# Four key-rounding steps moved from the end of a batch into the first three pairs of the next

## Chip, cores and metric

One Trainium2 chip, one core. The metric is the device time of one execution in microseconds, lower is better.

## What is computed

Two layers of gated cross-attention with a feed-forward part each, on x of 32 batches x 100 rows x 256, with a context of 32 x 1444 x 64. The change lies in the second layer's attention (sixteen heads), which per batch is, cut:

```python
kv_r = _apply_rope(kv_c, sin_k[None], cos_k[None])
q_r = jnp.einsum('bshq,hqr->bhsr', q_big, W_qr)
k_r = jnp.einsum('bld,hdr->bhlr', kv_r, W_kr)
scores = jnp.einsum('bhsr,bhlr->bhsl', q_r, k_r)
attn = jax.nn.softmax(scores, axis=-1)
ctx_c = jnp.einsum('bhsl,bld->bhsd', attn, kv_r)
```

The kernel folds W_kr into the queries, so that all heads share the 64-wide keys kv_r.

## The kernel before

The second attention (`phase_l1_attention`) runs eight groups of G = 4 batches. A group has a head, which makes the queries of its four batches and prepares batch 0's keys, and then a body in which four batches follow one another. In the body each batch has two chunks of 800 queries and twelve tiles of 120 or 121 keys in each chunk, so 24 tiles w, taken two at a time: 12 **pairs** per batch, here numbered 0 to 11. Pair p has the tiles 2p and 2p + 1. The text calls the four batches of a group 0 to 3, and the stretch between two of them a transition (into batch 1, 2 or 3).

All engines walk the same list of pairs, each with its own instruction stream, in the order written:

- **TensorE (PE)**, per pair: the scores of two tiles into c_s_ps (L1674 for the row maxima where r < 2, then L1676, L1678, L1680), a few "units" of the row maxima of the next batch (L1587), the values of the pair before (L1692), more units. Scores are three products, because each key is split in a rounded part k1 and a remainder k2, each held twice, on partitions 0 to 63 and on 64 to 127.
- **ScalarE (ACT)**, per pair: four exps c_s_ps to c_p (L1508); now and then the copies of the outputs (`drain`, L1473) and of the sums of the denominators (L1479); then, in two halves, the "rise" units of the maxima (L1456), with the **rounding steps** after the rises of the first half.
- **GpSimd (POOL)**, per pair: c_psum, the sum of the two exp tiles (L1194); at some pairs also the rotation of later keys (L1150, L1153, L1159) and the differences c_kd (L1174).
- **VectorE (DVE)**, per pair: the "low" and "mid" units of the maxima (L1271, L1277), then the accumulation of c_psum in c_acc (L1313, L1316), and at pairs 9, 10 and 11 one third of the split of the next keys (`split_keys`, L1267).

The maxima units come as rise, low and mid, each in one of three PSUM banks; TensorE may use a bank again when ScalarE (rise) or VectorE (low, mid) has read it. Exps of pair u wait for GpSimd's add of pair u - 2.

The nine rounding steps of a batch are in `round_steps` (L1458). Steps 0, 1, 2 write the rounded keys' three thirds to partitions 0 to 63 of k1, steps 3, 4, 5 the same to partitions 64 to 127 (both L1463, from c_kd); steps 6, 7, 8 copy the three thirds of the remainder k2 to the upper partitions (L1467), each after VectorE's L1267 for that third. The steps count up the semaphores k1_hi and k2_ready. `TILE_STEPS` (L971) says behind which tile of the batch before each step runs. Of those who wait: VectorE's third k waits for step k. TensorE's scores wait in `scores`, in the first chunk:

```python
if c == 0 and r % 4 == 0:
    pe.wait_ge(k1_hi, PRIMED + (it * G + j) * 6 + 4 + r // 4)
    pe.wait_ge(k2_ready, PRIMED + (it * G + j) * 3 + 1 + r // 4)
```

so the scores of pair 0 (r = 0) need steps 0 to 3 and 6, those of pair 2 (r = 4) steps 4 and 7, and those of pair 4 (r = 8) steps 5 and 8. `copy_keys` (L1440) overwrites c_kd with the next batch's keys, before the differences and the steps; it runs at pair 4 of batches 0 and 1, at pair 3 of batch 2, and in the head.

Of the kernel before, what the change touches and what calls it, by code (L numbers as in the profile page):

```python
# [15 lines left out]
G = 4  # L16
# [19 lines left out]
PRIMED = 1  # L36
# [3 lines left out]
def keys_of(r):  # L40
    return KP if r < 4 else KP - 1
# [796 lines left out]
def phase_l1_attention(nc, outer, sem, io, m):  # L838
# [12 lines left out]
    CT = CH * NT  # L851
    HEADS = [2 * i for i in range(H // 2)] + [2 * i + 1 for i in range(H // 2)]
    HALFQ, QUART = CQS // 2, CQS // 4
    with ExitStack() as ctx:
# [4 lines left out]
        def count(name):  # L859
            counters.append(sem(name))  # L860
            return counters[-1]
# [39 lines left out]
        kd_ready, k1_hi, k1_ready, k2_ready = count("c_kd_ready"), count("c_k1_hi"), count("c_k1_ready"), count("c_k2_ready")  # L901
# [15 lines left out]
        def beside_head(i):  # L917
            if i == HEAD_DEN:
                return ("den", -1)
            if i == HEAD_KEYS:  # L920
                return ("keys", 0)
            if i in HEAD_MAX:
                return ("max", 0, 0, HEAD_MAX.index(i))
            return ("none",)
# [43 lines left out]
        AFTER_PROJECT = {next_in(2, units_at(j, 15).start): j for j in range(1, G - 1)}  # L968

        HEAD_STEPS = {10: (0, 1), 11: (2,), 12: (3,), 13: (4, 5), 15: (6, 7, 8)}  # L970
        TILE_STEPS = {16: (0,), 17: (1,), 18: (2,), 19: (3,), 20: (4,), 21: (5,), 22: (6,), 23: (7,)}  # L971

        def pairs():
            for u in range(NP):
                yield u, u // BP, u // CP % CH, u % CP

        def head_cols(i):
            h = HEADS[i]
            return slice((h % 2) * CQS + (h // 2) * S, (h % 2) * CQS + (h // 2 + 1) * S)

        with nc.Block() as block:
# [448 lines left out]
            @block.scalar  # L1430
            def _(a):
                def copy_queries(gi, pair, src):
                    a.wait_ge(q_ps_ready, PRIMED + gi * (H // 2) + pair + 1)
                    a.sem_inc(m.carrier, 1)
                    for i in range(2):
                        for half in range(2):
                            a.activation(q1[half * DL:(half + 1) * DL, :, head_cols(2 * pair + i)],  # L1437
                                         src[i * DL:(i + 1) * DL, 0:T].rearrange("p (b s) -> p b s", b=G), ACT.Copy).then_inc(q1_ready, 1)

                def copy_keys(b):  # L1440
                    for k in range(3):
                        a.wait_ge(kt_ready, PRIMED + b * 3 + k + 1)
                        a.activation(kd[:, k * 4 * KP:(k + 1) * 4 * KP], m_ps[0:DL, k, 0:4 * KP], ACT.Copy).then_inc(kf_ready, 1)
                    a.activation(khigh[:, 0, :], m_ps[0:DL, 1, 0:4 * KP], ACT.Copy).then_inc(kmax_high, 1)

                def rise_tile(gi, t):
                    a.wait_ge(maxs_ready, PRIMED + gi * NMG + 3 * t + 3)
                    a.wait_ge(mneg_ready, PRIMED + gi * TG + t - 1)
                    a.activation(head_rises[t % 2], m_ps[:, 0, 0:4 * KP], ACT.Relu).then_inc(rise_ready, 1)

                def rise_unit(it, n):
                    j, k = divmod(n, NMU)
                    t, kind, half = UNITS[k]
                    a.wait_ge(maxs_ready, PRIMED + it * NMG + n + 1)
                    a.wait_ge(mneg_ready, PRIMED + it * TG + j * NMT + t - 1)
                    a.activation(rises[(j * NMT + t) % 2], m_ps[:, n % 3, 0:4 * KP], ACT.Relu).then_inc(rise_ready, 1)  # L1456

                def round_steps(b, j, n):  # L1458
                    cols = slice(n % 3 * 4 * KP, (n % 3 + 1) * 4 * KP)
                    if n < 6:  # L1460
                        a.wait_ge(kd_ready, PRIMED + (b + 1) * 5)
                        a.sem_inc(m.carrier, 1)
                        a.activation(k1[j % 2][n // 3 * DL:(n // 3 + 1) * DL, cols], kd[:, cols], ACT.Copy).then_inc(k1_hi, 1)  # L1463
                    else:
                        a.wait_ge(k1_ready, PRIMED + b * 3 + n - 5)
                        a.sem_inc(m.carrier, 1)
                        a.activation(k2[j % 2][DL:128, cols], k2[j % 2][0:DL, cols].bitcast(F32), ACT.Copy).then_inc(k2_ready, 1)  # L1467

                def drain(ch):

                    a.wait_ge(pv_done, PRIMED + (ch + 1) * NT)
                    a.wait_ge(ct_ready, PRIMED + ch)
                    a.activation(onum[:], o_ps[:, 0:HALFQ], ACT.Copy).then_inc(on_ready, 1)  # L1473

                def drain_sums(ch):
                    a.wait_ge(den_done, PRIMED + ch + 1)
                    a.wait_ge(den_loaded, 16 * ch)
                    a.sem_inc(m.carrier, 1)
                    a.activation(oden[:], m_ps[:, 0, 0:QUART], ACT.Copy).then_inc(od_ready, 1)  # L1479

                def head(gi, prev):
                    for i in range(H):
                        if i >= 3 and i % 2 == 1:
                            copy_queries(gi, i // 2 - 1, o_ps)
                        what, *at = beside_head(i)
                        if what == "den" and prev:
                            drain_sums(gi * G * CH - 1)
                        if what == "keys":
                            copy_keys(gi * G)
                        if what == "max":  # L1490
                            rise_tile(gi, at[2])
                        for n in HEAD_STEPS.get(i, ()):
                            round_steps(gi * G, 0, n)
                def group(it):
                    a.activation(warm[:], m.ident[0:1, 0:1], ACT.Exp)
                    for u, j, c, q in pairs():
                        ch, k = (it * G + j) * CH + c, keys_of(2 * q)
                        for w in range(2 * u, 2 * u + 2):
                            n = it * NU + w
                            for i in range(2):  # L1500
                                a.wait_ge(s_ready, PRIMED + 2 * n + i + 1)
                                if w >= 4:
                                    a.wait_ge(pv_done, PRIMED + n - 3)
                                    a.wait_ge(psum_ready, PRIMED + it * NP + u - 1)
                                else:
                                    a.wait_ge(pv_done, PRIMED + it * NU)
                                    a.wait_ge(psum_ready, PRIMED + it * NP)
                                a.activation(p[0:k, w % 4, i * HALFQ:(i + 1) * HALFQ], s_ps[0:k, (2 * w + i) % 4, 0:HALFQ], ACT.Exp).then_inc(exp_ready, 1)  # L1508
                        if (j, c) != (0, 0) and q == 0:
                            drain(ch - 1)  # L1510
                        for half in range(2):
                            for what, at in beside(j, u % BP * 2 + half):
                                if what == "absorb":
                                    copy_queries(it, H // 2 - 1, m_ps[:, 2, :])
                                if what == "den":
                                    drain_sums(it * G * CH + at)
                                if what == "keys":
                                    copy_keys(it * G + at)
                            for n in units_at(j, u % BP * 2 + half):
                                if UNITS[n % NMU][1] == "rise":  # L1520
                                    rise_unit(it, n)
                            if half == 0:
                                for w in range(2 * u, 2 * u + 2):
                                    for n in TILE_STEPS.get(w % CT, ()) if j + 1 < G else ():
                                        round_steps(it * G + j + 1, j + 1, n)
                                    if w % CT == 1 and j > 0:
                                        round_steps(it * G + j, j, 8)
                    drain((it * G + G) * CH - 1)

                head(0, False)  # L1530
                with a.Fori(0, NG - 1) as it:
                    group(it)
                    head(it + 1, True)
                group(NG - 1)
                drain_sums(B * CH - 1)

# [640 lines left out]
```

## Time and profile before

| | us |
|---|---|
| median of 3 runs | 3296.32 |
| lowest, highest | 3287.39, 3297.56 |
| the profiled execution | 3302.86 |
| its span (first to last instruction) | 3301.1 |

Busy shares of that span: TensorE 86%, its weight loads (PEld) 58%, VectorE 69%, ScalarE 50%, GpSimd 50%. The granted TensorE clock is 0.932 of full speed on average.

How to read it: times in the timeline are us from the start of the span. A row gives the start, the length from the first instruction of the row to the end of the last, the engine, the line of the kernel, what it writes and reads, and how many instructions the row holds. In brackets stands how long the engine was idle before the row and what ended that. "<-issue" means that nothing in the profile shows what it waited for. PEld rows are TensorE's weight loads; the load is the first thing of a matmul to start.

### The profile page before, as it was taken

What the parts mean: (1) busy time and instruction counts of PE and PEld (TensorE: products, weight loads), DVE (VectorE), ACT (ScalarE), POOL (GpSimd) and SP (SyncE); (2) the same over time, 40 slices, a digit from 0 to 9 for tenths busy, and PEclk for the clock granted to TensorE, in tenths of its full rate; (3) what the DMA queues carried; (4) which work ended last, traced back from release to release, by engine and by line L of the source; (5) the groups of instructions that cost most, each with busy time, mean ns of one, the idle gap of its engine ahead of it and who ended that gap; (6) DMA issues with size and microseconds to landing.
All of it is one profiled execution on the core that took longest, in us unless ns stands there. A gap on an engine that the chain in (4) does not pass through costs nothing. (4 is left out here: it accounts for less than half of the span.)

```text
span 3301.1 us, 62826 instructions
## 1 busy us (share of the span) xinstructions
PE 2836.6 (86%) x18352; PEld 1917.0 (58%) x18352; DVE 2270.5 (69%) x4122; ACT 1658.6 (50%) x3458; POOL 1637.5 (50%) x1196
## 2 busy tenths in 40 slices
PE   5999979999798998898998999899899899886335
PEld 4777769999665565565555555556556556553123
DVE  5777764454376686677677667768767667766887
ACT  2333222222146646646646655655664664664556
POOL 0000012322166656666666666665665666663566
PEclk9888879999899999999999999999999999998566
DMA  4000010000300101000000000010110000011100
GB/s 112 0 0 0 0 48 10 5 10 10 75 6 21 26 10 23 19 16 17 21 21 16 22 19 17 16 26 7 23 23 11 22 19 16 11 48 35 44 13 24
DMA packets 130264, 71.20 MB, mean 22 GB/s; under 512 B 83582, under 2 KB 124510, under 8 KB 129880
## 3 DMA queue, kind: packets, MB, share of 16 engines
q1 hardware_dynamic: 129944, 67.45, 8.2%
q8 instruction: 138, 2.26, 0.3%
q14 instruction: 182, 1.49, 0.1%
HBM read 56.95 MB, written 10.04 MB: 20 GB/s over the span
## 5 line engine op out<-in xcount | busy, mean ns | idle before, releaser
L1194 POOL TENSOR_TENSOR c_psum<-c_p 120x800 f32<-120x800 f32 (+1 forms) x384 | 770.8, 2013 | 558.8 <-ACT c_p L1508 240.1
L1508 ACT ACTIVATE c_p<-c_s_ps 120x400 f32<-120x400 f32 (+1 forms) x1536 | 650.5, 512 | 331.8 <-PE c_s_ps L1680 258.7
L1692 PE MATMUL c_o_ps<-c_p,c_val 120*64 120x400 f32 (+1 forms) x3072 | 605.1, 516 | 10.9 <-ACT c_onum L1473 10.9
L1271 DVE TENSOR_REDUCE c_mpart<-c_m_ps 128x1 f32<-128x484 f32 x416 | 271.4, 653 | 203.6 <-PE c_m_ps L1587 203.1
L1587 PE MATMUL c_m_ps<-c_kmax,c_q 64*128 64x484 f32 x1080 | 308.5, 437 | 98.6 <-DVE c_mpart L1271 63.6
L1316 DVE TENSOR_TENSOR c_acc<-c_acc,c_psum 120x800 f32<-120x800 f32 x256 | 319.3, 1247 | 59.9 <-POOL c_psum L1194 57.9
L1185 POOL TENSOR_TENSOR l_rr<-c_psum,l_rr 96x400 f32<-96x400 f32 x256 | 263.6, 1052 | 191.0 <-DVE l_rr L1338 190.9
L1692 PEld LDWEIGHTS c_o_ps<-c_p,c_val 120*64 120x64 f32 (+1 forms) x3072 | 188.8, 137 | 273.5 <-issue 159.7
L1676 PE MATMUL c_s_ps<-c_q,c_k 64*120 64x400 f32 (+1 forms) x1536 | 322.9, 370 | 1.8 <-ACT c_p L1508 1.8
L1623 PE MATMUL c_s_ps<-c_xt,l_a 128*96 128x400 f32 x1536 | 310.8, 352 | 9.7 <-DVE l_rr L1338 7.8
L1277 DVE CUSTOM_DVE_ANT_0 c_xt<-c_m_ps,c_xt,c_mpart 128x484 fp32r<-128x484 f32 x360 | 259.9, 722 | 86.0 <-DVE c_mpart L1271 42.1
L1587 PEld LDWEIGHTS c_m_ps<-c_kmax,c_q 64*128 64x128 f32 x1080 | 144.3, 187 | 288.3 <-issue 157.9
L1680 PE MATMUL c_s_ps<-c_q,c_k 64*120 64x400 f32 (+1 forms) x1536 | 302.1, 346 | 0.0
L1678 PE MATMUL c_s_ps<-c_q,c_k 64*120 64x400 f32 (+1 forms) x1536 | 301.6, 346 | 0.0
L1623 PEld LDWEIGHTS c_s_ps<-c_xt,l_a 128*96 128x96 f32 x1536 | 240.2, 162 | 88.7 <-issue 42.6
L528 POOL TENSOR_TENSOR b_act_lo<-b_act,b_act_hi 128x400 fp32r<-128x400 f32 x88 | 92.0, 1050 | 293.7 <-ACT b_act_hi L672 293.7
L717 PE MATMUL b_gu_ps<-b_xt,l_a 128*128 128x400 f32 x1056 | 212.9, 353 | 8.0 <-DVE b_gated L563 7.9
L1456 ACT ACTIVATE c_xt<-c_m_ps 128x484 fp32r<-128x484 f32 x360 | 193.9, 587 | 48.0 <-PE c_m_ps L1587 31.9
L717 PEld LDWEIGHTS b_gu_ps<-b_xt,l_a 128*128 128x128 f32 x1056 | 195.4, 194 | 12.2 <-DVE b_gated L563 12.0
L1676 PEld LDWEIGHTS c_s_ps<-c_q,c_k 64*120 64x120 f32 (+1 forms) x1536 | 163.0, 181 | 67.4 <-issue 37.5
L1437 ACT ACTIVATE c_q<-c_o_ps 64x400 fp32r<-64x400 f32 x224 | 112.0, 500 | 176.9 <-PE c_o_ps L1613 172.8
L1678 PEld LDWEIGHTS c_s_ps<-c_q,c_k 64*120 64x120 f32 (+1 forms) x1536 | 173.2, 182 | 4.0
(258 smaller groups left out, 5212.1 us busy)
## 6 DMA issues: line engine op xcount, KB each, us to landing
c_rdb<-l_denominators SPq DMA_DIRECT2D x128, 100.0 KB, 2.7
c_kv<-in_ctx SPq DMA_DIRECT2D x32, 360.0 KB
c_mrow<-c_mneg SPq DMA_DIRECT2D x288, 0.5 KB, 2.0
x_rows<-in_x SPq DMA_DIRECT2D x4, 800.0 KB
x_spill<-x_rows SPq DMA_DIRECT2D x8, 400.0 KB
l_xa<-x_spill SPq DMA_DIRECT2D x8, 400.0 KB
c_xr<-x_spill SPq DMA_DIRECT2D x32, 100.0 KB
x_spill<-c_xr SPq DMA_DIRECT2D x32, 100.0 KB
```

The costliest lines, as they stand in the source:

```text
L717: mm = pe.matmul(gu_ps[:, t % 2, j, 0:T], w[wi][:, k, t * 128:(t + 1) * 128], xt[x][:, k, :], start=(i == 0 and k == 0), stop=(i == 2 and ...
L1185: g.tensor_tensor(rot[:, i % 4, a, :], psum[0:HALF, i % 2, a * T:(a + 1) * T], rs[:, i % 2, (1 - a) * T:(2 - a) * T], ALU.add).then_inc(ro ...
L1194: g.tensor_tensor(psum[0:k, u % 2, :], p[0:k, 2 * u % 4, :], p[0:k, (2 * u + 1) % 4, :], ALU.add).then_inc(psum_ready, 1)
L1271: v.tensor_reduce(mpart[:, t:t + 1], m_ps[:, bank, 0:4 * KP], AX.X, ALU.max, negate=True).then_inc(mpart_ready, 1)
L1316: v.tensor_tensor(acc[0:k, :], acc[0:k, :], psum[0:k, q % 2, :], ALU.add).then_inc(acc_ready, 1)
L1508: a.activation(p[0:k, w % 4, i * HALFQ:(i + 1) * HALFQ], s_ps[0:k, (2 * w + i) % 4, 0:HALFQ], ACT.Exp).then_inc(exp_ready, 1)
L1587: pe.matmul(m_ps[:, n % 3, 0:4 * KP], q1[rows, j, q], kmax[rows, 1 if kind == "rise" else 0, :], start=True, stop=True).then_inc(maxs_read ...
L1623: mm = pe.matmul(wide_banks(i)[0:HALF, a, 0:T], m.a[w][:, k, HEADS[i], a * HALF:(a + 1) * HALF], xt[x][:, k, :], start=(q == 0 and k == 0) ...
L1676: pe.matmul(bank[i][0:k], k1[j % 2][side[i], keys], q1[side[i], j, q[i]], start=False, stop=False, skip_group_check=True)
L1678: pe.matmul(bank[i][0:k], k2[j % 2][side[i], keys], q1[side[i], j, q[i]], start=False, stop=False, skip_group_check=True)
L1680: pe.matmul(bank[i][0:k], k1[j % 2][side[i], keys], q2[side[i], j, c, :], start=False, stop=True, skip_group_check=True).then_inc(s_ready, 1)
L1692: mm = pe.matmul(o_ps[i * DL:(i + 1) * DL, 0:HALFQ], val[0:k, j % 2, r, :], p[0:k, w % 4, i * HALFQ:(i + 1) * HALFQ], start=(r == 0), stop ...
```

## The change

Steps 4, 7, 5 and 8 of a batch's keys go to the first three pairs of that batch itself; steps 0, 1, 2, 3 and 6 stay in the last four pairs of the batch before, one in pairs 8, 9 and 11 and two in pair 10. `copy_keys` gets a wait for all six k1 steps of the keys before. Batch 0's keys, which are rounded in the head, keep their steps.

```diff
-        TILE_STEPS = {16: (0,), 17: (1,), 18: (2,), 19: (3,), 20: (4,), 21: (5,), 22: (6,), 23: (7,)}
+        TILE_STEPS, LATE_STEPS = {16: (0,), 18: (1,), 20: (2,), 21: (3,), 23: (6,)}, {1: (4,), 3: (7,), 4: (5,), 5: (8,)}
...
                 def copy_keys(b):
+                    a.wait_ge(k1_hi, PRIMED + b * 6)
                     for k in range(3):
...
                                     for n in TILE_STEPS.get(w % CT, ()) if j + 1 < G else ():
                                         round_steps(it * G + j + 1, j + 1, n)
-                                    if w % CT == 1 and j > 0:
-                                        round_steps(it * G + j, j, 8)
+                                    for n in LATE_STEPS.get(w % CT, ()) if j > 0 else ():
+                                        round_steps(it * G + j, j, n)
```

| pair | 8 | 9 | 10 | 11 | 0 | 1 | 2 |
|---|---|---|---|---|---|---|---|
| steps before | 0, 1 | 2, 3 | 4, 5 | 6, 7 | 8 | | |
| steps after | 0 | 1 | 2, 3 | 6 | 4 | 7 | 5, 8 |

## Rows read from the trace of the kernel before

**Rows 1.** The page: its first line and the busy shares.

```profile
span 3301.1 us, 62826 instructions
PE 2836.6 (86%) x18352; PEld 1917.0 (58%) x18352; DVE 2270.5 (69%) x4122; ACT 1658.6 (50%) x3458; POOL 1637.5 (50%) x1196
```

**Rows 2.** Groups by line, whole span: count, busy us, mean ns, idle before, releasers.

```profile
L1267 DVE TENSOR_TENSOR c_k<-c_kd,c_k 64x484 fp32r<-64x484 f32 x96 | 91.2, 962 | 0.0
L1467 ACT ACTIVATE c_k<-c_k 64x484 fp32r<-64x484 f32 x96 | 54.7, 601 | 13.3 <-DVE c_k L1267 12.1
```

**Rows 3.** Timeline of ScalarE, pairs 8 to 11 of batch 2: start, length, row.

```profile
2173.30 1.11 ACT L1463 ACTIVATE c_k<-c_kd 64x484 fp32r<-64x484 f32 x2
...
2178.52 1.69 ACT L1508 ACTIVATE c_p<-c_s_ps 120x400 f32<-120x400 f32 x4 [0.83 <-PE c_s_ps L1680]
...
2186.49 0.60 ACT L1467 ACTIVATE c_k<-c_k 64x484 fp32r<-64x484 f32 x1 [1.73 <-DVE c_k L1267]
2187.12 1.06 ACT L1456 ACTIVATE c_xt<-c_m_ps 128x484 fp32r<-128x484 f32 x2
```

**Rows 4.** Timeline of ScalarE, pair 10 of batch 0 and ahead of pair 11 of batch 1.

```profile
2070.87 1.69 ACT L1508 ACTIVATE c_p<-c_s_ps 120x400 f32<-120x400 f32 x4 [1.02 <-POOL c_psum L1194]
...
2130.24 0.58 ACT L1456 ACTIVATE c_xt<-c_m_ps 128x484 fp32r<-128x484 f32 x1 [1.29 <-DVE c_mneg L1277]
```

**Rows 5.** Timeline of TensorE's weight loads, from batch 2 into batch 3.

```profile
2186.72 0.18 PEld L1587 LDWEIGHTS c_m_ps<-c_kmax,c_q 64*128 64x128 f32 x1 [1.08 <-DVE c_mpart L1271]
2187.24 0.19 PEld L1674 LDWEIGHTS c_s_ps<-c_mrow,c_first 64*121 64x121 f32 x2 [0.34 <-ACT c_k L1467]
```

**Rows 6.** Timeline of VectorE, pairs 9 to 11 of batch 2.

```profile
2178.96 1.67 DVE L1316 TENSOR_TENSOR c_acc<-c_acc,c_psum 120x800 f32<-120x800 f32 x1
2180.55 2.37 DVE L1267 TENSOR_TENSOR c_k<-c_kd,c_k 64x484 fp32r<-64x484 f32 x1
...
2185.45 0.65 DVE L1267 TENSOR_TENSOR c_k<-c_kd,c_k 64x484 fp32r<-64x484 f32 x1
```

**Rows 7.** Timeline of ScalarE and weight loads, pairs 1 to 3 of batch 1.

```profile
2088.38 1.70 ACT L1508 ACTIVATE c_p<-c_s_ps 121x400 f32<-121x400 f32 x4
...
2090.68 0.18 PEld L1676 LDWEIGHTS c_s_ps<-c_q,c_k 64*120 64x120 f32 x2 [0.32 <-issue]
...
2094.28 1.04 ACT L1456 ACTIVATE c_xt<-c_m_ps 128x484 fp32r<-128x484 f32 x2 [0.99 <-PE c_m_ps L1587]
2095.21 1.70 ACT L1508 ACTIVATE c_p<-c_s_ps 120x400 f32<-120x400 f32 x4
```

**Rows 8.** Timeline of ScalarE and weight loads, pairs 1 and 2 of batch 2.

```profile
2139.01 1.69 ACT L1508 ACTIVATE c_p<-c_s_ps 121x400 f32<-121x400 f32 x4
...
2141.64 0.18 PEld L1676 LDWEIGHTS c_s_ps<-c_q,c_k 64*120 64x120 f32 x2 [0.32 <-issue]
```

**Rows 9.** Timeline of ScalarE and weight loads, pairs 1 and 2 of batch 3.

```profile
2193.44 1.07 ACT L1456 ACTIVATE c_xt<-c_m_ps 128x484 fp32r<-128x484 f32 x2
...
2194.74 0.18 PEld L1676 LDWEIGHTS c_s_ps<-c_q,c_k 64*120 64x120 f32 x2 [0.32 <-issue]
```

**Rows 10.** Timeline of both, sixth group, from batch 0 into batch 1.

```profile
2344.88 1.10 ACT L1467 ACTIVATE c_k<-c_k 64x484 fp32r<-64x484 f32 x2
...
2345.88 0.19 PEld L1674 LDWEIGHTS c_s_ps<-c_mrow,c_first 64*121 64x121 f32 x2 [0.47 <-ACT c_k L1467]
```

**Rows 11.** Timelines of GpSimd and ScalarE, pairs 3 and 4 of batch 3.

```profile
2199.51 1.69 ACT L1508 ACTIVATE c_p<-c_s_ps 120x400 f32<-120x400 f32 x4 [2.10 <-POOL c_psum L1194]
...
2200.92 3.75 POOL L1194 TENSOR_TENSOR c_psum<-c_p 120x800 f32<-120x800 f32 x2 [1.44 <-DVE c_acc L1313]
...
2202.86 1.69 ACT L1508 ACTIVATE c_p<-c_s_ps 120x400 f32<-120x400 f32 x4 [1.66 <-POOL c_psum L1194]
```

**Rows 12.** Timelines of GpSimd and VectorE, pairs 2 to 4 of batch 1.

```profile
2095.73 3.76 POOL L1194 TENSOR_TENSOR c_psum<-c_p 120x800 f32<-120x800 f32 x2 [1.29 <-ACT c_p L1508]
...
2098.91 1.42 DVE L1316 TENSOR_TENSOR c_acc<-c_acc,c_psum 120x800 f32<-120x800 f32 x1
```

## The prediction

> **What bounds the kernel now.** Read first the page's busy shares [rows 1]: TensorE is busy 86% of the span, ScalarE 50%. So a ScalarE step that moves is worth nothing by itself; it counts only where TensorE is made to wait for it, or is let go by it. Next come the costs of the pieces, from the groups by line [rows 2]: a rounding step of the last kind (L1467, steps 6 to 8) is 0.60 us, and L1267, the VectorE split between them, has a mean of 0.96 us. Only L1467 has idle time before it worth naming, 13.3 us, nearly all on L1267.
>
> Then the timeline of one group of four batches, the fifth (it starts at 2030). The eight groups repeat each other within some tenths of a us, so a place in it counts eight times. Each group has three transitions that the change touches, into batches 1, 2 and 3; batch 0's keys are rounded in the head, which stays. I number the pairs of a batch 0 to 11. In every pair TensorE's scores come first, and ScalarE does its four exps, the rises of the first half, then the rounding steps, then the rises of the second half.
>
> **Part 1: fewer steps in the last four pairs.** Before, pairs 8 to 11 carry two steps each and pair 0 of the next batch one. After, pairs 8 and 9 carry one, pair 10 two, pair 11 one. Gone from the end are steps 4, 5 and 7, three steps. If ScalarE were the bound this would give 3 x 0.5 us (two steps in a row take 1.11 us, [rows 3], so the second adds 0.5) x 24 transitions = 36 us. The rows say that it is not:
> - Into batch 1: behind the steps of pair 9, the exps of pair 10 start after 1.02 us of idle time that GpSimd's c_psum add ended [rows 4]. A step less only makes such a wait longer. Gain 0.
> - Into batch 2: ScalarE has no idle time behind the steps of pairs 8 and 9, so it may win up to 0.5 us in each, but ahead of pair 11's exps it waits 1.29 us, in a rise of pair 10, for VectorE's c_mneg [rows 4]; what it won is spent there. 0.
> - Into batch 3: the exps of pair 9 may win up to one step, 0.5 us, but those of pair 10 wait 0.83 us for TensorE [rows 3]: 0. In pair 11 step 7 waits 1.73 us for L1267 and holds the rises behind it until 2187.12 [rows 3]. After the change step 7 is not there, and the first rise can go some 1.1 us sooner. It is nobody's last wait: TensorE's last maxima in that pair waited for VectorE's c_mpart (1.08 us) and the scores of pair 0 come directly behind, at 2187.24 [rows 5].
> Gain 0. If the exps of pair 9 that ScalarE now holds back were worth something, I bound it by 0.2 us a group, 1.6 us: the rows that follow them all name another engine. What hides the steps here is VectorE, whose split L1267 takes 2.37 us in place of 0.65 while GpSimd adds [rows 6]. The split of each third still finds its step done: step 1 now ends a pair ahead of L1267's second piece, step 2 likewise ahead of the third.
>
> The Trainium skill has a rule on this (SBUF — State Buffer, section "Who interferes with whom"): only VectorE and GpSimd share a port pair, the loser blocks wholly, and ScalarE has ports of its own. By that rule the moved copies can't slow L1267 or the GpSimd adds directly, and 0.65 against 2.37 us is a lock and not ScalarE's doing; they can only shift who meets whom, which is the second and fourth case below.
>
> **Part 2: step 4 in place of step 8 in pair 0.** The same engine, place and length. 0.
>
> **Part 3: step 7 in pair 1.** This is the new cost. TensorE's scores of pair 2 (r = 4) wait for the second k2_ready, which is step 7. Before, it was done a pair before the batch began. Now ScalarE reaches it only behind pair 1's exps, and TensorE starts pair 2's scores about there. The step starts 0.03 us behind its predecessor (2187.09 to 2187.12, [rows 3]), takes 0.61, and TensorE's weight load follows its end by 0.15 us (2187.24 against 2187.09, [rows 3, 5]): 0.79 us in all.
> - Into batch 1: exps end at 2088.38 + 1.70 = 2090.08; + 0.79 = 2090.87; TensorE's load ran at 2090.68 [rows 7]. Late by 0.19.
> - Into batch 2: 2139.01 + 1.69 + 0.79 = 2141.49; the load ran at 2141.64 [rows 8]. Late by 0, and ScalarE was idle there.
> - Into batch 3: two rises lie between exps and step (slot 2 of batch 3 has rises in its first half). They end at 2193.44 + 1.07 = 2194.51; + 0.79 = 2195.30; the load ran at 2194.74 [rows 9]. Late by 0.56.
> Queued behind that wait on TensorE are the scores, maxima and values of pair 2, and VectorE and GpSimd behind those. Sum 0.75 us a group, x 8 = 6.0 us. The lag from step to load isn't the same everywhere: the longest I find is 2345.88 - (2344.88 + 0.60) = 0.40 us [rows 10], which gives 0.44 + 0.10 + 0.81 = 1.35 us a group, 10.8 us; a lag of 0.05 would give 0.09 + 0 + 0.46, 4.4 us. I take the 0.15 since it is of the same wait in the same group.
>
> Does the delay last? Into batch 3 the exps of pair 3 wait for GpSimd anyway, which would hide it. But VectorE's L1313, which comes behind pair 2's maxima, moves with TensorE; GpSimd's add waits 1.44 us for it, and the exps of pair 4 wait 1.66 us for that add [rows 11]. So the 0.56 us goes around and stays. If instead it is absorbed there, 1.5 us of the 6.0 remain.
>
> **Part 4: steps 5 and 8 in pair 2.** Needed for pair 4's scores, one pair of slack. Into batch 1 they take 1.1 us where ScalarE was idle 0.99 us before its rises [rows 7], so with the 0.19 of part 3 the rises and pair 3's exps come some 0.3 us later. Pair 4's scores need only the first of those exps, and come a pair later; 0. Cover gone, it would be 0.3 x 8 = 2.4 us.
>
> **Part 5: the added wait in copy_keys** (for all six L1463 of the batch before). Behind it on ScalarE are the copies to c_kd, behind those L1257 and the next maxima. The sixth step ran in pair 2, copy_keys comes in pair 3 or 4, and already waits there for TensorE's transposes. 0; an instruction more, below 0.1 us x 32 = 3 us were it not covered, my bound from the 0.03 us between neighbours [rows 3].
>
> **The sum.** 0 + 0 + 6.0 + 0 + 0 on the profiled execution's 3302.9 us (3301.1 us of span and 1.8 around it): 3308.9. That execution lies 6.6 us above the median of the runs, 3296.3, so I state 3296.3 + 6.0 = 3302.3 us, +0.18%. About 0.3%, 10 us, is what a measurement of this kernel can tell from no change.
>
> **The rivals.**
> 1. *Absorbed.* The 0.56 us of batch 3 vanishes in the waits for GpSimd (2.10 us of idle time ahead of pair 3's exps, [rows 11]), and part 1's 1.6 us comes in: 3296.3 + 1.5 - 1.6 = 3296 us. Against it stands the chain over L1313.
> 2. *A split escapes GpSimd: faster.* In pair 10 of batch 2, L1267 starts at 2180.55 behind the accumulation L1316, which is 1.67 us long under GpSimd's rotation of keys; GpSimd's next add starts when pair 10's exps end, 2178.52 + 1.69 = 2180.21, and L1267 takes 2.37 us under it in place of 0.65 [rows 3, 6]. If pair 9's exps come sooner, so do GpSimd's add and rotation, and from 0.4 us on L1267 would be first. VectorE then runs ahead by 1.72 us, and TensorE waited for it. Price at most -1.72 x 8 = -13.8, with part 3's 6.0 against it -7.8: 3288.5 us. ScalarE can give at most the 0.5 us of one step, and only if the scores were ready that early.
> 3. *No relation.* The wait for step 7 is hidden, because TensorE spends the 0.32 us ahead of that load on its own waits [rows 7 to 9] and the step ends inside them: as 1, 3296 to 3298 us.
> 4. *An accumulation falls under GpSimd: slower.* Into batch 1, late steps 5 and 8 push pair 3's exps. GpSimd's adds of pairs 2 and 3 run in one piece of 3.76 us until 2099.49, and VectorE's L1316 at 2098.91 overlaps only the end, 1.42 us long [rows 12]. If pair 3's exps end later than 2097.6, against 2095.21 + 1.70 = 2096.91 now [rows 7], the second add moves on and the accumulation takes up to 2.4 us: +1.0 x 8 = 8 on the 6.0: 3310 us. I expect 0.3 us of push, and 0.55 with the longest lag, so it takes more than I count. The 0.40 us lag everywhere gives nearly the same time, 3307.
>
> **Numbers.** Forecast, +4 to +11: 0.52. Rivals 1 and 3 together: 0.20. Rival 2: 0.12, rival 4: 0.16. The range reaches from rival 2's end to a little past rival 4: 3288 to 3313. Faster by over 0.3%: 0.13, a part of rival 2 and of what I don't see in the meeting of VectorE and GpSimd. Slower by over 0.3%: 0.22, rival 4 and the top of the forecast. Within: 0.65.
>
> **What would show it.** In the profile after: TensorE's load L1676 of pair 2 into batches 1 and 3 released by ScalarE's L1467, with idle time up to 0.5 and 0.9 us in place of 0.32, and not into batch 2; step L1467 in pair 11 of batch 2 followed at once by rises with no second L1467; exps of pairs 9 and 10 into batch 1 still released by c_psum; L1267's mean near 0.96 us. Wrong if L1267 or L1316 has another mean (rivals 2, 4), if pairs 8 to 11 get shorter by over 0.3 us, or if pair 2 doesn't get longer.

## The result and the profile after

The changed kernel was timed against the one before three times, each time in runs interleaved on one chip.

| timing | after, median us | before, median us | ratio, 95% interval |
|---|---|---|---|
| first | 3307.11 | 3293.66 | 1.0040 [1.0021, 1.0058] |
| again | 3304.44 | 3294.78 | 1.0033 [1.0014, 1.0052] |
| third | 3305.47 | 3297.19 | 1.0029 [1.0017, 1.0041] |

So the change makes the kernel slower, by 0.3 to 0.4%. Over all three, 30 executions of after have a mean of 3305.2 us and 110 of the kernel before (the unchanged copy of the last experiment among them) one of 3295.6: +9.5 us, plus or minus 2.3. The forecast was 3302.3 us, +6.0. The time falls in the range, the sign and the mechanism are as forecast, and the size is at the edge: +0.18% was forecast, with the chance on "within 0.3%", and the first timing says 0.4%. That the mean loss lies in the forecast's +4 to +11 us is in part luck, since about half of it stands in no term of the sum, as shown below.

The page of after, its first line and the busy shares, answers to [rows 1]:

```profile
span 3310.5 us, 62858 instructions
PE 2841.8 (86%) x18352; PEld 1921.9 (58%) x18352; DVE 2268.8 (69%) x4122; ACT 1661.0 (50%) x3458; POOL 1637.7 (49%) x1196
```

No engine got more to compute: 32 instructions came in (the waits of `copy_keys`). TensorE is busy 5.2 us longer with the same 18352 matmuls, and ScalarE 2.4 us. The profiled execution took 3312.5 us against 3302.9, but two later profiles of the same kernel have spans of 3296.4 and 3296.7 us, under the 3301.1 of before. A span by itself says nothing at this size; where the time went has to be read pair by pair. Lines from 1441 on are one higher in after and in the kernels made from it (L1468 is the L1467 of the rows before), and three higher in splits_later and best_of_both.

Groups by line, whole span, as in [rows 2]:

```profile
L1267 DVE TENSOR_TENSOR c_k<-c_kd,c_k 64x484 fp32r<-64x484 f32 x96 | 91.2, 962 | 0.0
L1468 ACT ACTIVATE c_k<-c_k 64x484 fp32r<-64x484 f32 x96 | 56.0, 599 | 1.2
```

The split keeps its mean of 962 ns to the digit: no sign that a split changed its place against GpSimd. The remainder steps, though, lost nearly all their idle time, 13.3 us before and 1.2 now: step 7 no longer waits in pair 11. That gain is real and bought nothing, as part 1 said. ScalarE in pair 11 of batch 2 shows it, where [rows 3] had step 7 behind 1.73 us of idle time:

```profile
2189.06 0.61 ACT L1468 ACTIVATE c_k<-c_k 64x484 fp32r<-64x484 f32 x1
...
2190.95 0.57 ACT L1457 ACTIVATE c_xt<-c_m_ps 128x484 fp32r<-128x484 f32 x1 [1.28 <-PE c_m_ps L1588]
```

One step, and then ScalarE waits 1.28 us for TensorE instead: the idle time has only changed its cause.

Now the pairs that got longer. Batch 3, ScalarE and TensorE in pairs 0 to 2, which answers to [rows 9]:

```profile
2196.16 0.61 ACT L1464 ACTIVATE c_k<-c_kd 64x484 fp32r<-64x484 f32 x1
2196.79 1.69 ACT L1509 ACTIVATE c_p<-c_s_ps 121x400 f32<-121x400 f32 x4
2198.35 1.07 ACT L1457 ACTIVATE c_xt<-c_m_ps 128x484 fp32r<-128x484 f32 x2
2199.18 0.55 PE L1594 MATMUL c_m_ps<-c_acc,c_ones 121*32 121x200 f32 x8 [0.37 <-ACT c_xt L1457]
2199.44 0.60 ACT L1468 ACTIVATE c_k<-c_k 64x484 fp32r<-64x484 f32 x1
2200.10 0.18 PEld L1677 LDWEIGHTS c_s_ps<-c_q,c_k 64*120 64x120 f32 x2 [0.76 <-ACT c_k L1468]
```

Step 7 runs behind the rises, from 2199.44 to 2200.04, and the load of pair 2's scores follows 0.06 us later, with 0.76 us of idle time that step 7 ended; before it was 0.32 us of issue. Batch 1 and batch 2, the same places, answer to [rows 7, 8]:

```profile
2093.10 1.70 ACT L1509 ACTIVATE c_p<-c_s_ps 121x400 f32<-121x400 f32 x4
2094.82 0.61 ACT L1468 ACTIVATE c_k<-c_k 64x484 fp32r<-64x484 f32 x1
2095.49 0.18 PEld L1677 LDWEIGHTS c_s_ps<-c_q,c_k 64*120 64x120 f32 x2 [0.39 <-ACT c_k L1468]
...
2143.91 1.69 ACT L1509 ACTIVATE c_p<-c_s_ps 121x400 f32<-121x400 f32 x4
2145.63 0.61 ACT L1468 ACTIVATE c_k<-c_k 64x484 fp32r<-64x484 f32 x1
2146.55 0.18 PEld L1677 LDWEIGHTS c_s_ps<-c_q,c_k 64*120 64x120 f32 x2 [0.32 <-ACT c_k L1468]
```

In batch 1 the idle time grew by 0.07 us. In batch 2 it is 0.32 us as before, and step 7 had ended at 2146.24, 0.31 us ahead of the load: the row names it, but it didn't hold the load.

To compare whole kernels I took, for each pair, the time from its first scores (the L1676 matmul) to those of the next pair, as a difference to before, and of the eight groups the median. For most pairs this repeats to 0.01 or 0.02 us between executions, where the time of an execution scatters by some 6 us. Two pairs do not repeat: pair 11 of batch 0 (5.4 to 6.4 us within before, and 0.13 us less for the unchanged kernel) and pair 0 of batch 1 (3.7 to 4.3 us within before). Pair 11 has a column of its own and is in no sum; pair 0 is in the sums, and 0.1 us of it means nothing. For all kernels of this text, us a group (a dash: under 0.03), with the timed difference at the end (ratio minus one, times 3295; for after the three values). Two slow executions, one of 4_and_7_in_pair1 (4575 us) and one of the kernel before (3653 us), are in no ratio.

| kernel | batch 0 pair 11 | batch 1 pair 0 | pair 1 | pair 3 | batch 3 pair 0 | pair 1 | elsewhere | sum x 8 | timed, 95% |
|---|---|---|---|---|---|---|---|---|---|
| after (three profiles) | -0.24 to 0 | 0 to +0.03 | +0.07 | +0.07 | - | +0.45 | - | +4.8 | +9.6 to +13.2 |
| step7_back | -0.11 | -0.10 | - | +0.07 | - | - | - | -0.2 | +4.6 (-2 to +11) |
| wait_alone | -0.25 | -0.06 | - | - | - | - | +0.04 | -0.2 | -3.3 (-8 to +2) |
| only_7_8 | -0.11 | -0.08 | - | - | - | +0.32 | - | +1.9 | +4.9 (-1 to +11) |
| 4_and_7_in_pair1 | +0.38 | +0.04 | +0.35 | +0.07 | - | +0.82 | +0.16 | +11.6 | +16.5 (+11 to +22) |
| 4_and_7_in_pair0 | -0.24 | - | +0.28 | +0.07 | - | +0.49 | - | +6.7 | +7.6 (+3 to +12) |
| splits_later | -0.17 | -0.08 | +0.54 | +0.07 | +1.23 | +0.49 | -2.68 | -3.3 | -6.6 (-12 to -1) |
| rotation_later | -0.07 | -0.12 | - | - | +0.78 | - | +3.42 | +32.6 | +33 (+26 to +40) |
| step8_to_pair2 | -0.14 | - | - | - | - | -0.14 | - | -1.1 | +1.0 (-3 to +5) |
| best_of_both | -0.15 | +0.55 | - | - | - | -0.14 | -2.23 | -14.5 | -15.2 (-20 to -10) |
| same_again | -0.13 | - | - | - | - | - | - | 0 | +1.3 (-4 to +6) |

### The profile page after: what moved, and what is told of

The parts are those of the page before. It is cut to its first block and busy times, and to the rows that moved or that the text cites. A ratio compares the mean times of both kernels' runs of the same rounds, so it can differ in the third digit from the quotient of the medians.

```text
span 3310.5 us, 62858 instructions
## 1 busy us (share of the span) xinstructions
PE 2841.8 (86%) x18352; PEld 1921.9 (58%) x18352; DVE 2268.8 (69%) x4122; ACT 1661.0 (50%) x3458; POOL 1637.7 (49%) x1196
## 5 line engine op out<-in xcount | busy, mean ns | idle before, releaser
L1316 DVE TENSOR_TENSOR c_acc<-c_acc,c_psum 120x800 f32<-120x800 f32 x256 | 317.3, 1239 | 59.9 <-POOL c_psum L1194 57.9
```

The source lines that it names most:

```text
L1316: v.tensor_tensor(acc[0:k, :], acc[0:k, :], psum[0:k, q % 2, :], ALU.add).then_inc(acc_ready, 1)
```

## The experiments

Each edit is against the kernel before or the changed one, as its first line says. The pair numbers are those of the table above.

**After, again, and step 7 back in its place.** The first asks whether the pair times repeat; the second, whether step 7 alone carries them.

> The changed kernel once more. Theory A (step 7 holds TensorE back ahead of pair 2; nothing else costs): the two traces show 0.45 us into batch 3 and 0.07 to 0.2 us into batch 1, about 4.4 us in eight groups, so a ratio of 1.0013 to before; the 1.004 measured first was then partly chance. Theory B (a further cost that the one trace doesn't show): 1.004 again, some 13 us.

```diff
 against the changed kernel, step7_back:
-TILE_STEPS, LATE_STEPS = {16: (0,), 18: (1,), 20: (2,), 21: (3,), 23: (6,)}, {1: (4,), 3: (7,), 4: (5,), 5: (8,)}
+TILE_STEPS, LATE_STEPS = {16: (0,), 18: (1,), 20: (2,), 21: (3,), 22: (6,), 23: (7,)}, {1: (4,), 4: (5,), 5: (8,)}
```

> The changed kernel with step 7 alone back in pair 11 of the batch before. Theory A: the load of pair 2 into batch 3 returns to its old distance, pair 1 there 0.45 us shorter than in the changed kernel, total equal to before within 1 us. Theory B (fewer steps at the end, or the wait in copy_keys, cost): stays at +8 us or more.

After again: 1.0033 [1.0014, 1.0052], with pair 1 of batch 3 longer by 0.44 us (0.45 in the first profile) and pairs 1 and 3 of batch 1 by 0.07 each. Step 7 back: 3302.08 us, 1.0014 [0.9994, 1.0033], and in batch 3, pairs 1 and 2:

```profile
2194.05 0.55 PE L1594 MATMUL c_m_ps<-c_acc,c_ones 121*32 121x200 f32 x8 [0.37 <-ACT c_xt L1457]
2194.52 0.18 PEld L1677 LDWEIGHTS c_s_ps<-c_q,c_k 64*120 64x120 f32 x2 [0.32 <-issue]
```

The load waits for nothing that the profile shows, as before, and the 0.45 is gone to the last hundredth. The timing of this kernel, 1.0014 with an interval from 0.9994 to 1.0033, tells it neither from before nor from after. So the finding rests on the pairs, and after timed again, 1.0033, speaks for the further cost of theory B. What is left of the change, steps 4, 5 and 8 in the next batch, costs 0.07 us a group, in pair 3 of batch 1, which appears in every kernel that has both steps 5 and 8 in pair 2 and in no other. Step 7 in pair 1 makes up nearly all of what the pairs gained.

**The wait alone, and only the steps of the remainder.** wait_alone is before with the wait in `copy_keys` and nothing else; only_7_8 leaves steps 4 and 5 in the batch before.

```diff
 against the kernel before, wait_alone:
 def copy_keys(b):
+    a.wait_ge(k1_hi, PRIMED + b * 6)
```

```diff
 against the changed kernel, only_7_8:
+TILE_STEPS, LATE_STEPS = {16: (0,), 17: (1,), 18: (2,), 19: (3,), 20: (4,), 21: (5,), 22: (6,)}, {3: (7,), 5: (8,)}
```

> The kernel before with only the added wait in copy_keys. Theory A: 0, below 1 us. Theory B, if the wait is its cause: +3 to +10 us.

> The changed kernel with steps 0 to 6 where they were before and only 7 and 8 late, in pairs 1 and 2. Theory A: into batch 3 the same 0.45 us, into batch 1 the same 0.1 or less, so +3.5 to +4.5 us over before, like the changed kernel. Theory B, if the cost is in steps 4 and 5: nearer 0.

The wait alone: 3293.87 us, 0.9990 [0.9975, 1.0006], and no pair longer by more than 0.04 us. Part 5's nothing holds. Only 7 and 8: 3297.97 us, 1.0015 [0.9998, 1.0033]; into batch 3:

```profile
2186.67 0.55 PE L1594 MATMUL c_m_ps<-c_acc,c_ones 121*32 121x200 f32 x8 [0.24 <-ACT c_xt L1457]
2186.94 0.60 ACT L1468 ACTIVATE c_k<-c_k 64x484 fp32r<-64x484 f32 x1
2187.59 0.18 PEld L1677 LDWEIGHTS c_s_ps<-c_q,c_k 64*120 64x120 f32 x2 [0.77 <-ACT c_k L1468]
```

The load waits 0.77 us for step 7, as in after (0.76), yet the pair is only 0.32 us longer and not 0.45. The rest is in the line above it: with no step in pair 0, the exps and rises of pair 1 come sooner, and the denominators' matmul L1594 waits 0.24 us for a rise in place of 0.37. So a step in pair 0 isn't free in batch 3 either. My part 3 had not seen this; the next two runs follow it.

**Steps 4 and 7 together, in pair 1 or in pair 0.**

```diff
 against the changed kernel, 4_and_7_in_pair1:
-TILE_STEPS, LATE_STEPS = {...}, {1: (4,), 3: (7,), 4: (5,), 5: (8,)}
+TILE_STEPS, LATE_STEPS = {...}, {3: (4, 7), 4: (5,), 5: (8,)}
 and 4_and_7_in_pair0:
+TILE_STEPS, LATE_STEPS = {...}, {1: (4, 7), 4: (5,), 5: (8,)}
```

> The changed kernel with step 4 moved from pair 0 to pair 1, right ahead of step 7, so that step 7 ends half a us later. Theory A (step 7's end sets pair 2's start): pair 1 gets longer than in the kernel before by 0.45 + 0.5 = 0.95 us in batch 3, by 0.07 + 0.5 = 0.57 in batch 1, and by some 0.3 in batch 2, where the slack ends: 1.8 us a group, +14.6 us to before, +10 to the changed kernel. Theory C (the delay is absorbed further on once it grows): the sum over the group stays below 1 us, +8.

> The changed kernel with step 7 moved from pair 1 to pair 0, behind step 4. Theory A: step 7 ends a pair ahead of its use, so pair 1 of batch 3 is as long as before, though all else of the change stays: 0 to before, at most +0.1 us a group from the exps of pair 1 starting 0.5 us later. Theory B (thinner last pairs or late 5 and 8 cost): +5 to +9 us to before as the changed kernel.

In pair 1: 3314.82 us, 1.0050 [1.0032, 1.0067]. ScalarE and TensorE, batch 3:

```profile
2198.33 0.60 ACT L1464 ACTIVATE c_k<-c_kd 64x484 fp32r<-64x484 f32 x1
2198.84 0.59 ACT L1468 ACTIVATE c_k<-c_k 64x484 fp32r<-64x484 f32 x1
...
2199.48 0.18 PEld L1677 LDWEIGHTS c_s_ps<-c_q,c_k 64*120 64x120 f32 x2 [1.26 <-ACT c_k L1468]
```

Step 7 starts 0.51 us behind step 4, and the load's idle time goes from 0.76 to 1.26: exactly one step more. (The pair grows by 0.82 - 0.45 = 0.37 us only, since no step is left in pair 0, which gives back 0.13 as in only_7_8.) The wait is on the path, and in batch 3 an instruction ahead of step 7 counts in full at the load. In batches 1 and 2 the pair grew by 0.35 and 0.16 us where 0.57 and 0.3 were expected, so the +14.6 of theory A came out as +11.6 in the pairs; timed it is +16.5, 11 to 22. In pair 0: 3305.28 us, 1.0023 [1.0010, 1.0035]. If only the end of step 7 mattered, this kernel would have cost nothing in batch 3, since step 7 is over two us before pair 2. It cost 0.49:

```profile
2187.59 0.61 ACT L1464 ACTIVATE c_k<-c_kd 64x484 fp32r<-64x484 f32 x1
2188.10 0.59 ACT L1468 ACTIVATE c_k<-c_k 64x484 fp32r<-64x484 f32 x1
2188.71 1.69 ACT L1509 ACTIVATE c_p<-c_s_ps 121x400 f32<-121x400 f32 x4
2190.27 1.07 ACT L1457 ACTIVATE c_xt<-c_m_ps 128x484 fp32r<-128x484 f32 x2
2191.10 0.55 PE L1594 MATMUL c_m_ps<-c_acc,c_ones 121*32 121x200 f32 x8 [0.86 <-ACT c_xt L1457]
2191.57 0.18 PEld L1677 LDWEIGHTS c_s_ps<-c_q,c_k 64*120 64x120 f32 x2 [0.32 <-issue]
```

Read it from the bottom: the load of pair 2 waits for nothing, but the matmul ahead of it in TensorE's order waits 0.86 us for a rise, 0.49 more than before. The rise stands directly behind the exps of pair 1, those directly behind the steps. That chain has no gap, so a second step in pair 0 is paid there, and one in pair 1 at the load. The theory that only step 7's end counts has fallen, for batch 3; the one in its place is that ScalarE itself bounds the first two pairs of batch 3, at 0.45 to 0.5 us a step. The +0.28 us in pair 1 of batch 1 is a third place of the same kind. There a rise of pair 0 stands directly behind step 7, which ends at 2083.88, and TensorE's next maxima unit needs its bank:

```profile
2083.91 1.04 ACT L1457 ACTIVATE c_xt<-c_m_ps 128x484 fp32r<-128x484 f32 x2
...
2084.53 0.18 PEld L1588 LDWEIGHTS c_m_ps<-c_kmax,c_q 64*128 64x128 f32 x1 [0.47 <-ACT c_xt L1457]
```

In the kernel before, the same two loads run directly one behind the other.

**What the end of a batch could give: splits a pair later, rotation later.** Both ask whether VectorE's collisions with GpSimd, and not ScalarE, hold pairs 10 and 11. splits_later moves L1267 from pairs 9, 10, 11 to pairs 10, 11 and pair 0 of the next batch. rotation_later moves GpSimd's rotation of keys from pairs 7 and 8 to 9 and 10.

```diff
 against 4_and_7_in_pair0, splits_later:
-if j + 1 < G and c == 1 and q >= 3:
-    split_keys(it * G + j + 1, j + 1, (q - 3,))
+if j + 1 < G and c == 1 and q >= 4:
+    split_keys(it * G + j + 1, j + 1, (q - 4,))
+if j > 0 and (c, q) == (0, 0):
+    split_keys(it * G + j, j, (2,))
 against the kernel before, rotation_later:
-if (more or j + 2 < G) and j + 1 < G and at in (7, 8):
-    rotate_keys(b + 2, at - 7)
+if (more or j + 2 < G) and j + 1 < G and at in (9, 10):
+    rotate_keys(b + 2, at - 9)
```

> The kernel with steps 4 and 7 in pair 0, and VectorE's three splits L1267 one pair later (pairs 10, 11 and 0 of the next batch in place of 9, 10, 11). Theory D (the first split runs under GpSimd's adds at 2.3 us in place of 0.65 into batches 1 and 3, and TensorE's 4.3 us stall in pair 10 of batch 0 hangs on it): L1267's mean falls from 0.96 to some 0.65 to 0.7 us, pair 10 of batch 0 gets shorter by 1.7 us or more and pair 11 of batch 2 by some 1.5: -3.2 x 8 = -26 us. Rival E (VectorE is behind there for another cause, the slow L1316): under -5 us.

> The kernel before with GpSimd's first two pieces of the key rotation (L1150, L1153) at pairs 9 and 10 in place of 7 and 8. Theory D': they no longer delay the adds of pairs 8 and 9 into batch 1, L1316 there falls from 2.5 to 1.0 us and the first split to 0.65, pair 10 of batch 0 gets shorter by 3 us: -24 us. Rival: the rotation meets VectorE's second and third splits and the accumulations of pairs 10 and 11 instead, and the time stays within 5 us or rises.

Splits later: 3289.67 us, 0.9980 [0.9965, 0.9996], faster than the 1.0023 of the same kernel without the edit by some 14 us. Theory D is right on pair 10 of batch 0 and on the split's mean (697 ns), but its -26 us did not come: -6.6 was measured. In the kernel before, pair 10 of batch 0 (VectorE, then TensorE's weight load):

```profile
2073.38 2.32 DVE L1267 TENSOR_TENSOR c_k<-c_kd,c_k 64x484 fp32r<-64x484 f32 x1
...
2076.33 0.28 PEld L1587 LDWEIGHTS c_m_ps<-c_kmax,c_q 64*128 64x128 f32 x1 [4.57 <-DVE c_mpart L1271]
```

and in splits_later, the same pair:

```profile
2061.26 2.50 DVE L1316 TENSOR_TENSOR c_acc<-c_acc,c_psum 120x800 f32<-120x800 f32 x1 [0.67 <-POOL c_psum L1194]
...
2064.38 0.18 PEld L1590 LDWEIGHTS c_m_ps<-c_kmax,c_q 64*128 64x128 f32 x1 [2.34 <-DVE c_mpart L1271]
...
2068.13 0.65 DVE L1267 TENSOR_TENSOR c_k<-c_kd,c_k 64x484 fp32r<-64x484 f32 x1
```

The accumulation is caught under GpSimd's work in both (2.50 us here, against 1.48 for the next one); before, the split came directly behind it, under GpSimd's adds, and TensorE's maxima waited for both, 2.32 us for the split. A pair later it takes 0.65, and TensorE's stall falls from 4.57 to 2.34 us: -2.23 a group. Pair 0 of batch 3 gives half of it back, 1.23 us. Step 6 waits for its split in pair 11 of batch 2 there, but that isn't the cause. The rows are step 6, then the first load of batch 3, and windows over its scores (us, busy and count of PE, PEld, DVE, ACT, POOL, granted clock, DMA share, GB/s):

```profile
2174.17 0.60 ACT L1470 ACTIVATE c_k<-c_k 64x484 fp32r<-64x484 f32 x1 [1.66 <-DVE c_k L1267]
...
2175.20 0.18 PEld L1677 LDWEIGHTS c_s_ps<-c_mrow,c_first 64*121 64x121 f32 x2 [0.34 <-issue]
...
2176.00:2178.20 2.20, 2.20 (x14) 1.68 (x12) 1.71 (x3) 1.33 (x4) 0.00 (x0) 0.50 0.07 1
```

The load doesn't wait for step 6: it idles 0.34 us as in [rows 5]. The clock is what changed: TensorE had idled for 1.82 us in pair 11 (0.79 in the kernel before), waiting for VectorE's c_mpart, and its scores behind that run at 0.50 of full speed. In seven of the eight groups this pair has a granted clock of 0.66 to 0.74 and is 1.04 to 1.58 us longer; in the eighth the clock stays at 1.00 and the pair is 0.01 us longer.

Rotation later: 3330.68 us, 1.0100 [1.0079, 1.0121], so the rival was right and theory D' not. The rotation then meets the splits head on; the group L1267 of this kernel is

```profile
L1267 DVE TENSOR_TENSOR c_k<-c_kd,c_k 64x484 fp32r<-64x484 f32 x96 | 126.0, 1325 | 0.0
```

a mean of 1325 ns in place of 962, 34.8 us in all, and the timed difference is 33 us. That the two are so near is in part chance: pair 0 of batches 2 and 3 is 1.2 to 1.6 us longer in four of the eight groups each, some 11 us together, each time at a granted clock of 0.65 to 0.71; where the clock is 1.00, all but one of these pairs are as long as before. Who meets whom on VectorE and GpSimd counts for more here than where a rounding step stands. The Trainium skill (SBUF — State Buffer, section "Who interferes with whom") has these two engines share a port pair under an exclusive lock. The 0.65 against 2.32 us of this case agree with it.

**Step 8 from pair 0 to pair 2, by itself.** If ScalarE bounds the start of batch 3, then taking the one step of pair 0 away should win what adding one cost.

```diff
 against the kernel before:
-if w % CT == 1 and j > 0:
+if w % CT == 5 and j > 0:
     round_steps(it * G + j, j, 8)
```

> The kernel before with step 8 alone moved, from pair 0 to pair 2, so that no step lies in pairs 0 and 1. Theory F (in batch 3 ScalarE's own chain from the output copy through pair 1's exps and rises sets TensorE's denominators matmul, and every step in pairs 0 and 1 costs its 0.5 us there): the 0.37 us that this matmul waits for the rises goes, pair 1 of batch 3 is 0.37 us shorter than before, total -3 us (-0.1%). Theory A (only step 7's own end matters): no change, 0.

3298.93 us, 1.0003 [0.9991, 1.0015]. The pair did get shorter, by 0.14 us and not by the 0.37 that the matmul's wait would have allowed. Its rows, pairs 1 and 2 of batch 3:

```profile
2183.55 1.69 ACT L1508 ACTIVATE c_p<-c_s_ps 121x400 f32<-121x400 f32 x4 [0.51 <-PE c_s_ps L1680]
...
2185.94 0.55 PE L1593 MATMUL c_m_ps<-c_acc,c_ones 121*32 121x200 f32 x8 [0.23 <-ACT c_xt L1456]
2186.41 0.18 PEld L1676 LDWEIGHTS c_s_ps<-c_q,c_k 64*120 64x120 f32 x2 [0.32 <-issue]
```

The matmul still waits for the rise, 0.23 us. But the exps at the head of the chain now wait 0.51 us for TensorE's scores, where in the kernel before they came directly behind step 8; they start 0.81 us behind the pair's first scores in place of 0.95. So the step was the last to hold them by 0.14 us only: a step more costs its whole length, a step less wins 0.14. That is why a bound found by adding work may not be read backwards.

**The best of both.** The splits later only into batch 1, where they paid; elsewhere as before; step 8 in pair 2; step 7 in pair 1 of batch 1 alone, since its split comes later there.

```diff
 against the kernel before:
+LATE_STEPS = {5: (8,)}
+FIRST_STEPS, FIRST_LATE = {w: n for w, n in TILE_STEPS.items() if w < 23}, {3: (7,), 5: (8,)}
+SPLITS, FIRST_SPLITS = {3: (0,), 4: (1,), 5: (2,)}, {4: (0,), 5: (1, 2)}
...
-if j + 1 < G and c == 1 and q >= 3:
-    split_keys(it * G + j + 1, j + 1, (q - 3,))
+if j + 1 < G and c == 1:
+    split_keys(it * G + j + 1, j + 1, (SPLITS if j > 0 else FIRST_SPLITS).get(q, ()))
...
-for n in TILE_STEPS.get(w % CT, ()) if j + 1 < G else ():
+for n in (TILE_STEPS if j > 0 else FIRST_STEPS).get(w % CT, ()) if j + 1 < G else ():
     round_steps(it * G + j + 1, j + 1, n)
-if w % CT == 1 and j > 0:
-    round_steps(it * G + j, j, 8)
+for n in (LATE_STEPS if j > 1 else FIRST_LATE).get(w % CT, ()) if j > 0 else ():
+    round_steps(it * G + j, j, n)
```

> Into batch 1: VectorE's splits in pairs 10, 11, 11, step 7 in pair 1, step 8 in pair 2, the other steps as before; into batches 2 and 3 the kernel before with step 8 in pair 2. Theory D and F: pair 10 of batch 0 shorter by 2.2 us, pair 1 of batch 3 by 0.37, L1267's mean near 0.77 us; -2.6 us a group, -21 us. Rival: the two splits in pair 11 give back what pair 10 gains, -3 to -8 us.

3278.90 us, 0.9954 [0.9939, 0.9970]: faster than both kernels. Groups by line and the stall of pair 10, batch 0:

```profile
L1270 DVE TENSOR_TENSOR c_k<-c_kd,c_k 64x484 fp32r<-64x484 f32 x96 | 77.2, 823 | 0.0
...
2061.01 0.18 PEld L1590 LDWEIGHTS c_m_ps<-c_kmax,c_q 64*128 64x128 f32 x1 [2.35 <-DVE c_mpart L1274]
...
2067.18 0.18 PEld L1677 LDWEIGHTS c_s_ps<-c_mrow,c_first 64*121 64x121 f32 x2 [1.86 <-issue]
2067.19 0.45 PE L1677 MATMUL c_s_ps<-c_mrow,c_first 64*121 64x400 f32 x2 [1.57 <-DMA c_mrow<-c_mneg]
```

The pairs add to -14.5 us (8 x (-2.23 + 0.55 - 0.14)), the timing says -15.2. The 0.55 us in pair 0 of batch 1 is the median of a wide scatter, 0.85 us shorter to 0.84 us longer; with pair 11 ahead of it that stretch takes 9.94 us in the mean of the eight groups, against 10.00 and 9.94 in the two profiles of the unchanged kernel. The last two rows are its next limit: in three groups, this one among them, TensorE comes to the head of batch 1 so early that its first matmul waits 1.57 to 1.71 us for the DMA that brings the row maxima, c_mrow.

**The control, and after a third time.** The unchanged kernel before, timed as if it were a change, and the changed one once more beside it.

> The kernel before, unchanged, as a control for what the timing can tell: 0, ratio 1.000 with an interval of about 0.002. Were it 1.001 or more, the 5 us between the changed kernel's runs and its trace would lie in the way of comparing.

> The changed kernel a third time, beside the control. Theory A or F: the pairs of its trace sum to +4 to +5 us, ratio 1.0015. Theory B: +10 us again, 1.003, with the control at 1.000.

The unchanged kernel: 3297.01 us, 1.0004 [0.9989, 1.0019], all pair medians under 0.03 us but pair 11 of batch 0. After: 3305.47 us, 1.0029 [1.0017, 1.0041], pairs as in its other two profiles. So what the comparison adds by itself is below 0.2%, and after's 0.3% is not of that kind. Theory A is right on the pairs and theory B on the time: there is a further cost that the pairs don't show. The two also show a place outside the groups where they differ, told below.

## Why the prediction was right or wrong

- **Part 1, nothing from the end of the batch: right.** Pairs 8 to 11 differ by 0.03 us or less in all three profiles of after, pair 11 of batch 0 left aside, which doesn't repeat. Step 7's 1.73 us wait vanished and nobody was waiting for it.
- **Part 2, step 4 for step 8: right** as an exchange. But the reason was incomplete: a step there is free in batches 1 and 2 and costs some 0.13 us in batch 3 (0.45 with it, 0.32 without).
- **Part 3, step 7 in pair 1: the mechanism right, the term too large.** Forecast 0.19, 0 and 0.56 us; the pairs grew by 0.07, 0 and 0.45. The step that missed is the lag from the end of step 7 to TensorE's load: I took 0.15 from another wait in the same group, where the step wasn't what the load waited for (that load idles 0.34 us in after too, with step 7 gone: 2192.14, "0.34 <-issue"), and it is 0.06 in both rows where step 7 is the last wait (2094.82 + 0.61 to 2095.49, 2199.44 + 0.60 to 2200.10). My lower end, a lag of 0.05, was the right row: it gave 4.4 us, and the pairs 1 of batches 1 and 3 add to 4.2. In batch 2 it was absorbed as forecast. The loads idle 0.39 and 0.76 us where I had said "up to 0.5 and 0.9".
- **The delay persists: right.** Over pairs 2 to 10 of batch 3 nothing is given back, against rival 1. The chain that I named carries it: in [rows 11] GpSimd's add waited 1.44 us for L1313 and the exps of pair 4 waited 1.66 us for that add; in after it is 1.91 and 2.12, some 0.46 us longer each.
- **Part 4, steps 5 and 8: nearly right.** Forecast 0, upper bound 0.3 us a group; it was 0.07, in pair 3 of batch 1, 0.6 us in all.
- **Part 5, the wait: right in the groups**, 0.9990 [0.9975, 1.0006] alone. What it may do behind them is open.
- **The rivals.** 1 and 3 (absorbed, no relation) are out: pair 1 of batch 3 grew, and the load is released by step 7. 2 and 4 are out: L1267 has the same mean, and L1316 1239 ns in after's groups by line against 1247 before, 2.0 us less in all and not the 8 us more of rival 4. The mechanism of rival 2 exists all the same, by another lever: ScalarE could not free a split, moving the split did, and in pair 10 of batch 0 it gave 2.23 us, where I had priced one escape in batch 2 at 1.72.
- **The sum: too small by 3.5 us, plus or minus 2.3.** The pairs give 4.8 us where I forecast 6.0, and the kernel lost 9.5. So 4.7 us of the loss, plus or minus 2.3, are outside what the pair medians show, and no part of my sum has them. Two places are in the profiles. One is the tail, below: the stretch from the last pair to the end is 3.0 to 3.3 us longer in the three profiles of after than in the control (2.0 to 2.4 longer than in the first profile of before). The other is scattered: the sum over all pairs, instead of the medians, is 6.5 to 7.8 us over that of the control, but that of the first profile of before is 3.8 us over it too, so a part of it is the noise of one execution. I call the 4.8 us shown, since one edit (step 7 back) takes away 0.45 of the 0.6 us a group, and the tail seen but not explained.

Nearly half of the tail's difference is TensorE's last project, 16 matmuls behind 5 us of idle time. The control and the third profile of after, groups of that line:

```profile
3026.30 5.20 PE L1599 MATMUL c_m_ps<-l_cvo,c_ct 128*100 128x256 f32 x16 [5.04 <-DVE c_ct L1301]
```

```profile
3026.76 6.63 PE L1600 MATMUL c_m_ps<-l_cvo,c_ct 128*100 128x256 f32 x16 [5.12 <-DVE c_ct L1301]
```

The same matmuls behind the same wait take 1.43 us longer; the rest of the difference lies behind them, in the feed-forward part, and was not followed. Windows over them (columns: us, busy and count of PE, PEld, DVE, ACT, POOL, granted clock, DMA share, GB/s), first the control, then after:

```profile
3026.30:3029.50 3.20, 3.20 (x8) 2.24 (x9) 3.02 (x6) 0.00 (x0) 0.00 (x0) 0.52 0.00 0
3029.50:3031.50 2.00, 2.00 (x10) 1.23 (x8) 0.89 (x4) 0.00 (x0) 0.00 (x0) 1.00 0.00 0
```

```profile
3026.70:3032.50 5.80, 5.74 (x14) 4.01 (x15) 3.97 (x9) 0.00 (x0) 0.00 (x0) 0.50 0.00 0
```

In the control TensorE is granted 1.2 GHz for 3.2 us and then 2.4; in after 1.2 GHz for 5.8. All nine profiles of kernels with the wait in `copy_keys` have 5.99 to 6.69 us there. Of the five without it, four have 5.09 to 5.40, and rotation_later has 6.12. That looks like a relation, but I know no way from that wait to this place, and the kernel with the wait alone has the long project (its tail, too, is 3.1 us over the control's) and no cost in its timed runs. It stays open.

## What to carry to other kernels

Moving a step off an engine that waits anyway gains nothing where another engine releases the work behind it, and it costs as soon as the step becomes the last thing that a bounding engine waits for; ask of the new place first, not of the old. Price that wait with the lag of the same pair of engines, and look not only at who waits for the moved step but also at what stands behind it on its own engine: the chain steps, exps, rises, denominators cost as much as the wait itself. Where two engines slow each other, moving one of the two instructions can be worth more: the kernel that did it here won 15 us, 1 of them by step 8. Look then at what the stall did to the clock, too, and at what comes last once the stall is gone.

## What the hardware showed that I had not expected

**A stall is paid a second time in clock, the short one too, but less.** The kernel before, batch 0 into batch 1, in two windows (columns as above): the stall and the 4 us behind it. Then best_of_both around its shorter stall, in the same group:

```profile
2072.10:2076.30 4.20, 0.00 (x0) 0.00 (x0) 4.17 (x3) 2.13 (x5) 4.20 (x3) 0.75 0.00 0
2076.30:2080.30 4.00, 3.83 (x16) 2.77 (x16) 3.34 (x7) 1.49 (x4) 1.14 (x1) 0.50 0.08 13
```

```profile
2060.90:2066.00 5.10, 4.19 (x26) 2.28 (x26) 4.41 (x9) 3.38 (x8) 4.07 (x3) 1.00 0.14 39
```

In this group TensorE works at 0.50 of full speed, 1.2 GHz, for 4 us behind 4.2 us of idling, and at 1.00 behind the shorter stall. The first holds in all eight groups of before (0.50 or 0.51 over the 4 us behind the stall). The second doesn't: in best_of_both three groups keep 1.00 and five have 0.50 to 0.79, and in splits_later, with a stall of the same length, all eight have 0.53 to 0.75. The clock falls at another moment in each group, in before from 1.6 to 4.3 us after the stall began, so another share of the low stretch falls on work. Pair 11 of batch 0 takes anything between 5.4 and 6.6 us for it, in before as in after (5.41 and 6.56 us in the same group of the two first profiles). Whether the shorter stall saves time there too isn't shown: the median of pair 11 is 0.15 us lower in best_of_both, and 0.13 us lower in the unchanged kernel.

**An instruction's neighbour sets its length, not its size.** The same VectorE split of 64 x 484 takes 0.65 us alone and 2.32 under GpSimd's adds, the accumulation of 120 x 800 takes 2.50 us in pair 10 of splits_later and 1.48 in pair 11.

**Executions scatter more than the programs differ.** The stretch ahead of the first pair, in which at most one wait differs, was between 7.2 us shorter and 6.3 us longer than in the control. Three profiles of after have spans of 3310.5, 3296.4 and 3296.7 us, with the pairs that repeat the same to 0.03 us in the median. The 4.8 us of this change can be read in the trace from a single execution, by place, and a loss of 5 to 10 us in the time only from dozens; and the two need not agree, as here.
